# Attention with exponentials over three PSUM banks, transposes on VectorE and projections inside the loop

## The chip, the cores and the metric

The kernel runs on one core of a Trainium2 chip. The metric is the time of one launch in device microseconds (us). The engines are named as in the profile: PE (TensorE, with PEld for its weight loads), DVE (VectorE), ACT (ScalarE), POOL (GpSimd) and SP (the queue that issues most DMAs). Each engine runs its own instructions in order and waits on semaphores for the others. SBUF holds the data, PSUM (8 banks of 512 fp32 columns in each of 128 partitions) takes what PE computes.

## The reference

Six sublayers follow each other on an input x of 2 x 1024 x 128; only the first three matter here.

```python
x = x + 0.5 * _L0_ffn_ref(_layernorm(x), ...)    # routed cross attention
x = x + _L0_attn_ref(_layernorm(x), W_kqv, W_proj, q_norm_w, k_norm_w)
x = x + 0.5 * _L0_ffn_ref(_layernorm(x), ...)    # the same layer again
x = x + 0.5 * _L1_ffn_ref(...); x = x + _L1_attn_ref(...); x = x + 0.5 * _L1_ffn_ref(...)

# _L0_attn_ref, B=2, T=1024, H=16 heads of D=8
scores = jnp.einsum('bhtd,bhsd->bhts', q, k) / jnp.sqrt(jnp.float32(D))
scores = jnp.where(causal[None, None], -jnp.inf, scores)
att = jax.nn.softmax(scores, axis=-1)
y = jnp.einsum('bhts,bhsd->bhtd', att, v)
return y.transpose(0, 2, 1, 3).reshape(B, T, C) @ W_proj.T

# _L0_ffn_ref: the rows that each of 4 groups works on are chosen by a router
q_top, q_idx = jax.lax.top_k(q_logits, NQ);   queries = x[bidx, q_idx]
kv_top, kv_idx = jax.lax.top_k(kv_logits, NK); key_values = x[bidx, kv_idx]
```

## The kernel before

The program is written by hand: each engine has a list of instructions in a fixed order, and semaphores between them. `kinds` lists the sublayers; `attn(i)` and `ffn(i)` exist once for each engine. `ps` is the whole PSUM.

**The attention loop.** For each batch entry b (2) and each group hg of four heads (4), twelve steps run in the order of `ORDER` (L347). A step is one block of 128 keys (kt) against one half of the queries (qc, 512 of them), for four heads. Blocks on the causal diagonal are narrower: 512, 384, 256 or 128 queries (`SPAN`). There are 8 such groups of 12 steps. In a step:

- PE computes the scores (L1854, key on the partition, query along the row), two heads side by side on 64 rows each. They go to PSUM in fills of two banks, and three sets of two banks (banks 0 to 5) take turns. A full step has two fills, a narrow one (256 or 128) one.
- ACT takes the exponential of a fill (L1450) into the tile `P`, which holds 3 steps of 4 x 512. It waits for the scores of that fill and for the product three steps earlier (`pvs`), which frees its place.
- POOL zeroes what the causal mask forbids in diagonal blocks (L563).
- PE multiplies with the values (L1871), four heads side by side on 32 columns each, and adds up in bank 6 or 7. The values carry a column of ones, so the sum of the exponentials comes with it.

Here and below I call L1871 the product of a step. PE issues the scores two steps ahead: scores(s+2), then the product of s. When a unit (b, hg, qc) is complete, DVE copies its bank out (L1203), PE transposes it back (L1878), and DVE divides by the sums (L1206, L1208) into `Y`. After the loop, the four chunks of 512 tokens are transposed by PE (L1893), copied by ACT (L1453), projected by PE (L1898), and DVE adds them to X (L1215) and takes the statistics of the rows (L638, L641), one chunk after the other. The next layer starts from these.

**The gather in ffn.** The chosen rows are gathered by matmuls with one-hot matrices S. For each of 16 tiles of 128 tokens, DVE makes the 4 x 128 columns of the queries by comparing (L782), from `iota1` and `posT`, both in SBUF. The 4 x 64 columns of the keys take three instructions: a difference on POOL (L501), then an absolute value (L1324) and a relu (L1319) on ACT. PE waits for both and runs four matmuls (L1669): two parts of x, each against the queries and the keys.

Of the kernel before, what the change touches and what calls it, by code (L numbers as in the profile page):

```python
# [83 lines left out]
def _tiles():  # L84
    wide, order = 0, []
    for n in range(NNARROW):
        order.append((HT * NWIDE + n, 1))
        for _ in range(RUNS[n] if n < len(RUNS) else 0):
# [28 lines left out]
by_act = lambda t: t % 2 == 1  # L117
SIGNALS = {
# [3 lines left out]
                xn_high=2 * NC, xn_parts=NC, posTs=1, kdiff=NT, kabs=NT, Sk=NT, sig=2),  # L122
# [6 lines left out]
def build(nc, a, out, n_sub, start=0):  # L129
    ctx = ExitStack()  # L130
    with ctx:
# [77 lines left out]
        def rounded(name, at_word, shape):  # L209
# [64 lines left out]
        v = carve(head + [("P", 3 * HG * HALF), ("yT", 2 * HALF), ("Y", NT * D), ("tmp", 2 * P),  # L274
                          ("mx", 3 * TB * AH), ("msp", 3 * T // 2), ("mrest", T), ("rc", 2 * 16)])
        Pa = v["P"].rearrange("p (i h q) -> p i h q", i=3, h=HG)
        yT = v["yT"].rearrange("p (i q) -> p i q", i=2)
        Y = v["Y"].rearrange("p (t d) -> p t d", t=NT)
        YT = v["P"][:, 0:B * T]
        tmp = v["tmp"].rearrange("p (i q) -> p i q", i=2)  # L280
        mx = v["mx"].rearrange("p (k t h) -> p k t h", k=3, t=TB)
        rc = v["rc"].rearrange("p (i t h) -> p i t h", i=2, t=4)
# [64 lines left out]
        ORDER = ((0, 0), (1, 0), (0, 1), (1, 1), (0, 2), (1, 2), (0, 3), (1, 3), (1, 7), (1, 4), (1, 6), (1, 5))  # L347
        assert sorted(ORDER) == [(qc, kt) for qc in range(QC) for kt in range(4 * qc + 4)]
        STEPS = [(b, hg, qc, kt, all(q != qc for q, _ in ORDER[n + 1:]))
                 for b in range(B) for hg in range(NHG) for n, (qc, kt) in enumerate(ORDER)]  # L350
        SPAN = [HALF - P * max(0, kt - 4 * qc) for _, _, qc, kt, _ in STEPS]
        TURNS = [[(0, 1)] if n <= HALF // 2 else [(0,), (1,)] for n in SPAN]
        FILLS = [sum(len(x) for x in TURNS[:n]) for n in range(len(STEPS) + 1)]
        DIAG = [sum(kt >= 4 * qc for _, _, qc, kt, _ in STEPS[:n]) for n in range(len(STEPS) + 1)]
        ENDS = [n + 1 for n, x in enumerate(STEPS) if x[4]]
        UNIT = [sum(x[4] for x in STEPS[:n]) for n in range(len(STEPS) + 1)]

# [117 lines left out]
        def _(pool):  # L475
# [4 lines left out]
            def ffn(i):  # L480
# [16 lines left out]
                for t in range(NT):  # L497
                    if t >= 8:
                        pool.wait_ge(*at("Sk", i, t - 7))
                    j, r = spot(t)  # L500
                    nc.gpsimd.tensor_tensor(KD[:, t % 8], iota1[:, 0:NK].unsqueeze(1).broadcast_to([P, G, NK]),  # L501
                                            posT[:, j, r + G:r + 2 * G].unsqueeze(2).broadcast_to([P, G, NK]),
                                            ALU.subtract).then_inc(sem("kdiff", i), 1)
# [47 lines left out]
            def attn(i):  # L551
# [6 lines left out]

                for s_, (b, hg, qc, kt, last_) in enumerate(STEPS):
                    if kt >= 4 * qc:  # L560
                        pool.wait_ge(*at("exp", i, FILLS[s_ + 1]))
                        blk = Pa[:, s_ % 3, :, 0:P]
                        nc.gpsimd.affine_select(out=blk, in_=blk, pattern=[[0, HG], [1, P]], compare_op=ALU.is_ge,  # L563
                                                fill=0.0, base=0, channel_multiplier=-1).then_inc(sem("causal", i), 1)
# [60 lines left out]
        def _(dve):  # L625
# [89 lines left out]
            def ffn(i):  # L715
# [64 lines left out]
                for t in range(NT):  # L780
                    j, r = spot(t)
                    nc.vector.tensor_tensor(  # L782
                        S[:, t // TB, t % TB, 0:G * NQ].rearrange("p (g s) -> p g s", g=G),
                        iota1.unsqueeze(1).broadcast_to([P, G, NQ]),
# [290 lines left out]
            def attn(i):  # L1075
# [122 lines left out]
                for u in range(UNIT[-1]):  # L1198
                    b, hg, qc = u // (NHG * QC), u // QC % NHG, u % QC
                    dve.wait_ge(*at("pvs", i, ENDS[u]))  # L1200
                    if u >= 2:
                        dve.wait_ge(*at("yTt", i, u - 1))
                    nc.vector.tensor_copy(yT[:, u % 2, :], ps[:, 6 + u % 2, :]).then_inc(sem("yT", i), 1)  # L1203
# [8 lines left out]
                for c in range(NC):  # L1212
# [5 lines left out]
                    if i < last:  # L1218
                        row_stats(c, i + 1)
# [950 lines left out]
```

## Time and profile before

| | us |
|---|---|
| median of 3 runs | 814.76 (814.21 to 816.13) |
| profiled execution, its own time | 813.59 |
| its span in the trace | 811.8 |
| attention loop, first exponential to the end of the last | 170.8 to 309.0 |
| gather of the first ffn, its matmuls | 47.8 to 63.8 |
| gather of the second ffn, its matmuls | 357.6 to 373.5 |

The span is what the instructions of the trace cover; 1.8 us lie around it. Busy times of an engine count overlapping instructions once. A row of the timeline merges consecutive instructions of one line. Because instructions are pipelined, one starts before the end of the last, so what one more of them costs is read from the distance of two starts and not from its duration.

### The profile page before, as it was taken

What the parts mean: (1) busy time and instruction counts of PE and PEld (TensorE: products, weight loads), DVE (VectorE), ACT (ScalarE), POOL (GpSimd) and SP (SyncE); (2) the same over time, 40 slices, a digit from 0 to 9 for tenths busy, and PEclk for the clock granted to TensorE, in tenths of its full rate; (3) what the DMA queues carried; (4) which work ended last, traced back from release to release, by engine and by line L of the source; (5) the groups of instructions that cost most, each with busy time, mean ns of one, the idle gap of its engine ahead of it and who ended that gap; (6) DMA issues with size and microseconds to landing.
All of it is one profiled execution on the core that took longest, in us unless ns stands there. A gap on an engine that the chain in (4) does not pass through costs nothing. (4 is left out here: it accounts for less than half of the span.)

```text
span 811.8 us, 13446 instructions
## 1 busy us (share of the span) xinstructions
PE 641.5 (79%) x4710; PEld 468.1 (58%) x4710; DVE 459.0 (57%) x1401; ACT 441.7 (54%) x847; POOL 336.2 (41%) x422
## 2 busy tenths in 40 slices
PE   6879777479999998049877599999729758999990
PEld 3757574222222224036567589999628747999980
DVE  7894859931111115985747545556556783555572
ACT  5565534579999995536544444444424373444440
POOL 1173343203332221256150657765431046677553
PEclk9689999569999999559998789999959967999996
DMA  8220000668000000002000576667330028666654
GB/s 327 95 73 35 1 2 0 207 213 305 6 2 1 2 1 1 1 4 104 1 1 8 148 252 217 214 190 203 110 103 1 1 63 291 209 217 194 192 162 161
DMA packets 36470, 87.60 MB, mean 108 GB/s; under 512 B 5169, under 2 KB 20145, under 8 KB 35377
## 3 DMA queue, kind: packets, MB, share of 16 engines
q1 hardware_dynamic: 31280, 76.13, 28.5%
q0 software_dynamic: 5120, 10.58, 4.6%
q8 instruction: 39, 0.64, 0.3%
q14 instruction: 31, 0.25, 0.1%
HBM read 69.75 MB, written 16.94 MB: 107 GB/s over the span
## 5 line engine op out<-in xcount | busy, mean ns | idle before, releaser
L1959 PE MATMUL ps<-arena 128*128 128x256 f32 (+1 forms) x768 | 156.8, 356 | 2.3 <-issue 1.2
L1505 ACT ACTIVATE arena<-ps,arena 128x256 f32<-128x256 f32 (+1 forms) x192 | 84.1, 438 | 129.1 <-issue 76.5
L1959 PEld LDWEIGHTS ps<-arena 128*128 128x128 f32 x768 | 129.9, 196 | 19.0 <-issue 3.4
L1450 ACT ACTIVATE arena<-ps 128x1024 f32<-128x1024 f32 (+2 forms) x160 | 135.8, 957 | 4.0 <-PE ps L1854 2.6
L975 DVE SCALAR_TENSOR_TENSOR arena<-ps,arena 128x256 f32<-128x256 f32 (+1 forms) x192 | 84.3, 440 | 82.3 <-ACT arena L1505 80.4
L611 POOL DMA_INDIRECT yd<-arena,wqk x80 | 78.6, 983 | 68.5 <-DVE arena L997 57.5
L575 POOL DMA_INDIRECT arena<-xs,wqk x80 | 77.6, 970 | 31.4 <-issue 15.2
L563 POOL TENSOR_SCALAR_AFFINE_SELECT arena<-arena 128x512 f32<-128x512 f32 x64 | 40.6, 635 | 111.8 <-ACT arena L1450 111.8
L1871 PE MATMUL ps<-arena 128*32 128x512 f32 (+3 forms) x768 | 83.3, 506 | 2.7 <-DVE arena L1208 1.6
L1970 PE MATMUL ps<-arena 128*128 128x128 f32 x640 | 79.5, 275 | 2.0 <-DVE arena L997 2.0
L1970 PEld LDWEIGHTS ps<-arena 128*128 128x128 f32 x640 | 75.2, 192 | 2.5 <-issue 2.4
L1203 DVE COPY arena<-ps 128x512 f32<-128x512 f32 x16 | 11.1, 692 | 96.6 <-PE ps L1871 96.6
L1854 PE MATMUL ps<-arena 64*128 64x512 bf16 (+3 forms) x384 | 52.9, 338 | 8.9 <-DVE arena L1132 4.2
L1854 PEld LDWEIGHTS ps<-arena 64*128 64x128 bf16 x384 | 13.5, 94 | 66.5 <-ACT arena L1450 48.6
L501 POOL TENSOR_TENSOR arena<-consts,arena 128x256 f32<-128x256 f32 x32 | 32.8, 1061 | 23.5 <-DVE arena L774 23.5
L1563 PE MATMUL ps<-consts 128*128 128x128 f32 x146 | 26.2, 361 | 18.1 <-DVE X L1009 16.4
L1563 PEld LDWEIGHTS ps<-consts 128*128 128x128 f32 x146 | 25.1, 271 | 18.6 <-DVE X L1009 16.6
L993 DVE TENSOR_TENSOR arena<-ps,arena 128x256 f32<-128x256 f32 (+1 forms) x48 | 18.3, 380 | 26.1 <-PE ps L1970 25.7
L1871 PEld LDWEIGHTS ps<-arena 128*32 128x32 f32 x768 | 15.7, 108 | 30.0 <-issue 15.2
L782 DVE TENSOR_TENSOR S<-consts,arena 128x512 fp32r<-128x512 f32 x32 | 32.0, 1072 | 0.1
L1256 ACT ACTIVATE Xn<-X,rt 128x128 f32<-128x128 f32 x72 | 29.0, 479 | 1.2 <-DVE rt L693 1.2
L581 POOL TENSOR_SCALAR wvo<-wqk,wvo 128x24 f32<-128x24 f32 x2 | 0.7, 356 | 67.9 <-DVE wvo L928 67.9
(297 smaller groups left out, 1184.6 us busy)
## 6 DMA issues: line engine op xcount, KB each, us to landing
arena<-in_wall SPq DMA_DIRECT2D x48, 836.0 KB, 4.6
arena<-slots SPq DMA_DIRECT2D x2, 2048.0 KB, 7.2
arena<-scr_q SPq DMA_DIRECT2D x8, 512.0 KB, 6.6
arena<-scr_k SPq DMA_DIRECT2D x8, 512.0 KB, 7.7
arena<-yd SPq DMA_DIRECT2D x8, 512.0 KB, 5.5
xs<-Xn SPq DMA_DIRECT2D x8, 260.0 KB, 5.2
scr_q<-arena SPq DMA_DIRECT2D x4, 384.0 KB, 4.4
scr_k<-arena SPq DMA_DIRECT2D x4, 384.0 KB, 4.0
```

Of the source, the lines that this page charges most:

```text
L501: nc.gpsimd.tensor_tensor(KD[:, t % 8], iota1[:, 0:NK].unsqueeze(1).broadcast_to([P, G, NK]), posT[:, j, r + G:r + 2 * G].unsqueeze(2).bro ...
L563: nc.gpsimd.affine_select(out=blk, in_=blk, pattern=[[0, HG], [1, P]], compare_op=ALU.is_ge, fill=0.0, base=0, channel_multiplier=-1).then ...
L575: nc.gpsimd.indirect_dma_start(out=xt[:, slot, h, :], out_offset=None, in_=xs, in_offset=bass.IndirectOffsetOnAxis(ap=tokidx[:, col + h:co ...
L611: nc.gpsimd.indirect_dma_start(out=yd, out_offset=bass.IndirectOffsetOnAxis(ap=dest[:, col + h:col + h + 1], axis=0), in_=y_[:, slot, h, : ...
L975: nc.vector.scalar_tensor_tensor(out=hT[:, j % 2, f, 0:rows], in0=ps[:, 3 + k % 3, 0:rows], scalar=raw[:, slot, EW_BB + f:EW_BB + f + 1], ...
L1450: nc.scalar.activation(dst, src, ACT.Exp, scale=AD ** -0.5).then_inc(sem("exp", i), 1)
L1505: nc.scalar.activation(sl[:, k % 3, 0:rows], ps[:, k % 3, 0:rows], ACT.Silu, bias=raw[:, slot, EW_BA + f:EW_BA + f + 1]).then_inc(sem("sil ...
L1563: mm(ps[:, bank, 0:P], ident, ident, start=True, stop=True)
L1854: ins = mm(ps[:, 2 * (k % 3) + par, n * x:n * (x + 1)], Ks[64 * par:64 * par + R_ALL, h2, T * b + P * kt:T * b + P * (kt + 1)], Qs[64 * pa ...
L1871: ins = mm(ps[32 * j:32 * j + 32, 6 + u % 2, q0:HALF], Va[:, TB * b + kt, VW * h:VW * h + 32], Pa[:, s_ % 3, j, 0:HALF - q0], start=(kt == ...
L1959: ins = mm(ps[:, bank, 0:rows], raw[:, slot, w + P * f:w + P * (f + 1)], xTt[:, j % 2, 0:rows], start=True, stop=True)
L1970: ins = mm(ps[:, 6, D * h:D * (h + 1)], hT[:, j % 2, f, P * h:P * (h + 1)], raw[:, slot, EW_2 + D * f:EW_2 + D * (f + 1)], start=(f == 0), ...
```

## The change

Four things change in attention.

- Steps may hold two key blocks. `ORDER` has ten steps for each group, and the blocks 384+128 wide share a step. Each step takes whole banks of 512 columns: four banks, or two where the block is 256 wide. The 36 banks of a group are filled in 12 fills of three banks, regardless of where a step ends. Two sets of three banks (0 to 2, 3 to 5) take turns.
- One ACT instruction takes the exponential of 3 x 512 columns; there are 96 instead of 160. The tile `P` is as large as before, now a ring of 12 banks. `FREED` says how many products must be done before a fill may be written into it.
- PE issues scores(k+2), which wait for exponential k to be complete, and after them the products of the steps whose last bank was in fill k-1.
- A finished unit is transposed by DVE in blocks of 32 x 32, from PSUM to SBUF (L1242), divided there, and once the last group of heads is in, DVE transposes the blocks back (L1252) into the operand of the projection; the rows of W_proj are permuted on the host to match. PE transposes nothing in attention, ACT copies nothing after the loop. Chunks 0, 1 and 2 are projected and added to X inside the loop, at places given by `PROJECT_AFTER`; chunk 3 after it.

In ffn, PE puts `iota1` into PSUM bank 6, and DVE compares from there. For three of the 16 tiles (4, 9, 14) DVE makes the key columns too, so POOL and ACT make 13.

```diff
+KEYS_DVE = (4, 9, 14)
+KEYS_ACT = [t for t in range(NT) if t not in KEYS_DVE]
...
-        ORDER = ((0, 0), (1, 0), (0, 1), (1, 1), (0, 2), (1, 2), (0, 3), (1, 3), (1, 7), (1, 4), (1, 6), (1, 5))
...
+        ORDER = ((0, (0,)), (0, (1, 3)), (1, (0,)), (1, (1,)), (0, (2,)), (1, (6,)), (1, (4,)), (1, (2,)), (1, (5, 7)), (1, (3,)))
...
+        FILL, RING = 3, 3 * HG
+        NFILL = len(BANKS) // FILL
+        SCORE_FILLS = 6 // FILL
...
+        LAST_FILL = [max(n for n, (m, _) in enumerate(BANKS) if m == s_) // FILL for s_ in range(len(STEPS))]
+        FREED = [sum(n <= FILL * k + FILL - 1 - RING for n in FIRST_BANK) for k in range(NFILL)]
...
+        ADD_AT = [QC * NHG - 2, QC * NHG, UNITS - 2, UNITS - 1]
+        PROJECT_AFTER = [min(ENDS[u] + 3, len(STEPS) - 1) for u in ADD_AT[:-1]]
...
                     nc.vector.tensor_tensor(
                         S[:, t // TB, t % TB, 0:G * NQ].rearrange("p (g s) -> p g s", g=G),
-                        iota1.unsqueeze(1).broadcast_to([P, G, NQ]),
+                        ps[:, 6, 0:P].unsqueeze(1).broadcast_to([P, G, NQ]),
...
-                    nc.vector.tensor_copy(yT[:, u % 2, :], ps[:, 6 + u % 2, :]).then_inc(sem("yT", i), 1)
...
+                    nc.vector.transpose(yq[:, u % 2, :], ps[:, 6 + u % 2, :]).then_inc(sem("yq", i), 1)
...
+                        nc.vector.transpose(YT[:, HALF * c:HALF * (c + 1)], yn[:, qc, :]).then_inc(sem("YT", i), 1)
+                    if u in ADD_AT:
+                        add_projected(ADD_AT.index(u))
...
-                for s_, (b, hg, qc, kt, last_) in enumerate(STEPS):
-                    n = SPAN[s_]
-                    for k, us in enumerate(TURNS[s_], FILLS[s_]):
-                        act.wait_ge(*at("sT", i, k + 1))
-                        if s_ >= 3:
-                            act.wait_ge(*at("pvs", i, s_ - 2))
...
+                for k in range(NFILL):
+                    act.wait_ge(*at("sT", i, k + 1))
+                    if FREED[k]:
+                        act.wait_ge(*at("pvs", i, FREED[k]))
+                    n0, bank = FILL * k % RING, FILL * (k % SCORE_FILLS)
+                    nc.scalar.activation(Pa[:, n0:n0 + FILL, :], ps[:, bank:bank + FILL, :], ACT.Exp, scale=AD ** -0.5
+                                         ).then_inc(sem("exp", i), 1)
...
+                def scores(k):
+                    banks = BANKS[FILL * k:FILL * (k + 1)]
+                    if k >= SCORE_FILLS:
+                        pe.wait_ge(*at("exp", i, k - SCORE_FILLS + 1))
...
+                for k in range(SCORE_FILLS):
+                    scores(k)
+                for k in range(NFILL):
+                    if k + SCORE_FILLS < NFILL:
+                        scores(k + SCORE_FILLS)
+                    for s_ in range(len(STEPS)):
+                        if LAST_FILL[s_] == k - 1:
+                            attend(s_)
+                for s_ in range(len(STEPS)):
+                    if LAST_FILL[s_] == NFILL - 1:
+                        attend(s_)
+                attended(NC - 1)
```

**PE inside the loop**, at the change from the first group of heads to the second. `ps<-arena 128x512` is a score matmul, `ps<-arena 32x512` one of a product. Before, a step's scores, with a wait for an exponential at each fill of two banks, stand between two products:

```order
L1871 MATMUL ps<-arena 32x512 [waits attn_exp]
L1871 MATMUL ps<-arena 32x512 x3
L1854 MATMUL ps<-arena 128x128 [waits attn_exp]
L1854 MATMUL ps<-arena 128x128 x3
L1871 MATMUL ps<-arena 32x256 [waits attn_causal,attn_exp]
L1871 MATMUL ps<-arena 32x256 x3
L1854 MATMUL ps<-arena 128x512 [waits attn_exp]
L1854 MATMUL ps<-arena 128x512
```

Of the changed kernel, PE in the same place:

```order
L1889 MATMUL ps<-arena 128x512 [waits attn_exp]
L1889 MATMUL ps<-arena 128x512 x2
L1889 MATMUL ps<-arena 128x512 [waits attn_stack_01,attn_exp]
L1889 MATMUL ps<-arena 128x512 x2
L1912 MATMUL ps<-arena 32x512 [waits attn_exp]
L1912 MATMUL ps<-arena 32x512 x3
L1889 MATMUL ps<-arena 128x512 [waits attn_exp]
L1889 MATMUL ps<-arena 128x384 x2
L1889 MATMUL ps<-arena 128x128 x2
L1912 MATMUL ps<-arena 32x384 [waits attn_causal,attn_exp]
L1912 MATMUL ps<-arena 32x384 x3
L1912 MATMUL ps<-arena 32x128 x4
```

A score fill is now three matmuls (or more, narrow ones) behind one wait, and sometimes two fills stand between two products. No product stands between the wait for exponential k and the scores of fill k+2; the products come behind them.

**ACT at the start of the loop**, before:

```order
L1450 ACTIVATE arena<-ps 128x1024 [waits attn_sT,attn_split]
L1450 ACTIVATE arena<-ps 128x1024 [waits attn_sT] x3
L1450 ACTIVATE arena<-ps 128x2x384 [waits attn_sT] x2
L1450 ACTIVATE arena<-ps 128x1024 [waits attn_pvs,attn_sT] x2
L1450 ACTIVATE arena<-ps 128x2x2x256 [waits attn_pvs,attn_sT]
```

and of the changed kernel, with what stands ahead of the loop:

```order
L1452 ACTIVATE arena<-ps,attw 128x512 [waits attn_kqT]
L1456 ACTIVATE arena<-arena 128x512 [waits attn_rest] x2
L1483 ACTIVATE arena<-ps 128x1536 [waits attn_sT,attn_split]
L1483 ACTIVATE arena<-ps 128x1536 [waits attn_sT] x3
L1483 ACTIVATE arena<-ps 128x1536 [waits attn_pvs,attn_sT] x92
```

Four forms of two banks have become one form of three banks. Both wait for `pvs`; the number that it waits for is in `FREED`.

**PE behind the loop**, before, from the last product to the first transposes of the next layer (the pair of rows L1893 and the pair L1898 stand four times each):

```order
L1871 MATMUL ps<-arena 32x384 [waits attn_causal,attn_exp]
L1871 MATMUL ps<-arena 32x384 x3
L1878 MATMUL ps<-consts,arena 128x128 [waits attn_yT]
L1878 MATMUL ps<-consts,arena 128x128 x3
L1893 MATMUL ps<-consts,arena 128x128 [waits attn_Y]
L1893 MATMUL ps<-consts,arena 128x128 x3
```

and of the changed kernel:

```order
L1912 MATMUL ps<-arena 32x512 [waits attn_exp]
L1912 MATMUL ps<-arena 32x512 x3
L1920 MATMUL ps<-attw,arena 128x128 [waits attn_yq,attn_YT]
L1920 MATMUL ps<-attw,arena 128x128 x3
L1589 MATMUL ps<-consts,X 128x128 [waits x_chunk]
L1589 MATMUL ps<-consts,X 128x128 x3
```

One projection is left behind the last product, and directly after it the 16 transposes of the next layer.

## Rows read from the trace of the kernel before

**Rows 1.** The page of the profile: the costliest group of ACT: busy us, mean ns | idle before.

```profile
L1450 ACT ACTIVATE arena<-ps 128x1024 f32<-128x1024 f32 (+2 forms) x160 | 135.8, 957 | 4.0 <-PE ps L1854 2.6
```

**Rows 2.** Windows: stretch, length, busy us of each engine (instructions), granted clock, DMA.

```profile
170.00:178.30 8.30, 7.19 (x32) 1.13 (x32) 0.00 (x1) 6.86 (x8) 1.27 (x2) 0.50 0.90 290
178.30:309.00 130.70, 125.16 (x1176) 34.16 (x1172) 18.61 (x45) 128.92 (x153) 38.70 (x61) 1.00 0.18 62
...
196.00:213.10 17.10, 16.32 (x154) 4.46 (x152) 2.48 (x6) 16.93 (x21) 5.08 (x8) 1.00 0.44 162
```

**Rows 3.** ACT in the attention loop: start, duration, line, tile, forms, count.

```profile
170.77 5.18 ACT L1450 ACTIVATE arena<-ps 128x1024 f32<-128x1024 f32 x6 [1.49 <-PE ps L1854]
...
179.02 129.98 ACT L1450 ACTIVATE arena<-ps 128x1024 f32<-128x1024 f32 x152 [0.46 <-PE ps L1854]
...
201.38 0.61 ACT L1450 ACTIVATE arena<-ps 128x512 f32<-128x512 f32 x1
...
201.86 1.05 ACT L1450 ACTIVATE arena<-ps 128x1024 f32<-128x1024 f32 x1
...
207.10 1.06 ACT L1450 ACTIVATE arena<-ps 128x1024 f32<-128x1024 f32 x1
...
208.00 1.07 ACT L1450 ACTIVATE arena<-ps 128x1024 f32<-128x1024 f32 x1
```

**Rows 4.** PE in one group: start, duration, line, tile, count, idle before it.

```profile
205.67 0.61 PE L1854 MATMUL ps<-arena 64*128 64x512 bf16 x4
206.21 0.64 PE L1871 MATMUL ps<-arena 128*32 128x256 f32 x8
...
209.13 0.34 PE L1854 MATMUL ps<-arena 64*128 64x384 bf16 x2 [0.39 <-ACT arena L1450]
209.39 1.07 PE L1871 MATMUL ps<-arena 128*32 128x512 f32 x8
210.39 0.66 PE L1878 MATMUL ps<-consts,arena 128*128 128x128 f32 x4
```

**Rows 5.** The timeline behind the loop: DVE and PE.

```profile
310.76 0.69 DVE L1203 COPY arena<-ps 128x512 f32<-128x512 f32 x1 [3.93 <-PE ps L1871]
...
312.20 0.26 DVE L1206 RECIPROCAL arena<-ps 128x16 f32<-128x16 f32 x1 [0.75 <-PE ps L1878]
...
312.49 0.29 DVE L1208 TENSOR_TENSOR arena<-ps,arena 128x128 f32<-128x128 f32 x1
...
313.77 3.74 PE L1898 MATMUL ps<-attw,arena 128*128 128x128 f32 x32
...
320.99 0.69 DVE L1215 TENSOR_TENSOR X<-X,ps 128x512 f32<-128x512 f32 x1
...
325.95 0.42 DVE L726 TENSOR_TENSOR arena<-arena,ps 128x256 f32<-128x256 f32 x1 [0.29 <-ACT arena L1284]
```

**Rows 6.** The gather: timeline of the second ffn, L782 in the first, L1093, a window.

```profile
354.41 16.00 DVE L782 TENSOR_TENSOR S<-consts,arena 128x512 fp32r<-128x512 f32 x16
354.46 16.42 POOL L501 TENSOR_TENSOR arena<-consts,arena 128x256 f32<-128x256 f32 x16 [17.79 <-DVE arena L774]
...
L782 DVE TENSOR_TENSOR S<-consts,arena x15: 1095/1097/1101, 45.3 to 59.5; 128x512 fp32r<-128x512 f32 x15
...
L782 DVE TENSOR_TENSOR S<-consts,arena x2: 691/896/1101, 44.6 to 45.3; 128x512 fp32r<-128x512 f32 x2
...
L1093 DVE TENSOR_TENSOR arena<-ps,consts x16: 410/414/426, 127.9 to 155.6; 128x256 f32<-128x256 f32 x16
...
357.50:362.50 5.00, 4.91 (x15) 4.26 (x16) 5.00 (x6) 4.03 (x10) 5.00 (x6) 0.50 0.01 3
...
363.45 0.53 PE L1669 MATMUL ps<-S,xn_high 128*128 128x512 f32 x2
...
363.81 0.51 PE L1669 MATMUL ps<-S,xn_low 128*128 128x512 f32 x2
...
373.01 0.51 PE L1669 MATMUL ps<-S,xn_low 128*128 128x512 f32 x2
```

More of the change, by code:

```diff
@@ L351, in build @@
[L351 to L354, printed above, removed]
+        ORDER = ((0, (0,)), (0, (1, 3)), (1, (0,)), (1, (1,)), (0, (2,)), (1, (6,)), (1, (4,)), (1, (2,)), (1, (5, 7)), (1, (3,)))
+        assert sorted((qc, kt) for qc, kts in ORDER for kt in kts) == [(qc, kt) for qc in range(QC) for kt in range(4 * qc + 4)]
@@ new lines, in build @@
+        STEPS = [(b, hg, qc, kts, all(q != qc for q, _ in ORDER[n + 1:]))
+                 for b in range(B) for hg in range(NHG) for n, (qc, kts) in enumerate(ORDER)]
+        first_query = lambda qc, kt: P * max(0, kt - 4 * qc)
+        span = lambda qc, kt: HALF - first_query(qc, kt)
+        BANKS = []
+        for s_, (b, hg, qc, kts, last_) in enumerate(STEPS):
+            if span(qc, kts[0]) == HALF // 2:
+                BANKS += [(s_, [(par, kts[0], 0), (2 + par, kts[0], HALF // 2)]) for par in range(2)]
+            else:
+                BANKS += [(s_, [(j, kt, span(qc, kts[0]) * n) for n, kt in enumerate(kts)]) for j in range(HG)]
@@ L557, in attn @@
                     nc.gpsimd.tensor_tensor(kq[:, t, :], kq[:, t, :], rot[:, t % 2, :], ALU.add).then_inc(sem("kq", i), 1)
-                for s_, (b, hg, qc, kt, last_) in enumerate(STEPS):
[L560 to L564, printed above, removed]
+                for s_, (b, hg, qc, kts, last_) in enumerate(STEPS):
+                    if masked(s_):
+                        pool.wait_ge(*at("exp", i, LAST_FILL[s_] + 1))
+                        half = span(qc, kts[0]) == HALF // 2
+                        n0 = FIRST_BANK[s_] % RING
+                        for n in range(len(kts)):
+                            col = 3 * P * n
+                            blk = (Pa[:, n0:n0 + 2, :].rearrange("p j (u q) -> p (j u) q", u=2)[:, :, 0:P] if half
+                                   else Pa[:, n0:n0 + HG, col:col + P])
+                            ins = nc.gpsimd.affine_select(out=blk, in_=blk, pattern=[[0, HG], [1, P]], compare_op=ALU.is_ge,
+                                                          fill=0.0, base=0, channel_multiplier=-1)
+                        ins.then_inc(sem("causal", i), 1)
             def moe(i):
@@ L1665, in ffn @@
                         pe.wait_ge(*at("S", i, t + 1))
[L1666 removed]
+                        pe.wait_ge(*at("Sk", i, sum(m <= t for m in KEYS_ACT)))
                         for part in range(2):
@@ L1869, in pv @@
[L1869 to L1872 removed]
+                    if 0 in kts and u >= 2:
+                        pe.wait_ge(*at("yq", i, u - 1))
+                    if 0 in kts and u - 2 in ADD_AT:
+                        pe.wait_ge(*x_of(i + 1, ADD_AT.index(u - 2)))
@@ new lines, in pv @@
+                    where = {(j, kt): (FIRST_BANK[s_] % RING + x, col)
+                             for x, (m, pieces) in enumerate(BANKS[FIRST_BANK[s_]:FIRST_BANK[s_] + HG]) if m == s_
+                             for j, kt, col in pieces}
+                    for kt in kts:
+                        for j in range(HG):
+                            h = HG * hg + j
+                            n, col = where[j, kt]
+                            ins = mm(ps[32 * j:32 * j + 32, 6 + u % 2, first_query(qc, kt):HALF], Va[:, TB * b + kt, VW * h:VW * h + 32],
+                                     Pa[:, n, col:col + span(qc, kt)], start=(kt == 0), stop=last_ and kt == kts[-1])
```

175 lines of the change are left out of this document (79 added, 96 removed).

## The prediction

> **What bounds the kernel now.** I read the costliest groups first. The exponentials are 160 instructions and 135.8 us busy [rows 1], one sixth of the span. Then the windows: from 178.3 to 309.0 us ACT is busy 128.92 of 130.70 us, PE 125.16 [rows 2]. In one group of heads (196.0 to 213.1) ACT has 16.93 of 17.10 us, PE 16.32 [rows 2]. So ACT sets the pace of the loop and PE follows closely. The loop runs from 170.77 to 179.02 + 129.98 = 309.00 us, 138.2 us [rows 3].
>
> What does one exponential cost? Two of 1024 columns start 0.90 us apart (207.10, 208.00), one of 512 columns is followed after 0.48 (201.38, 201.86) [rows 3]. The difference, 0.42 us for 512 columns, is 0.83 ns a column; what is left for an instruction is 0.05 us. The duration of one is longer, 1.05 to 1.07 us at 1024 and 0.61 at 512 [rows 3]: it goes on in the pipeline after the next has begun, and only its end releases the others.
>
> **Attention loop: ACT's part.** The columns stay the same (18,432 for a group, 147,456 in all). At three banks an exponential starts every 0.90 + 0.42 = 1.32 us (I take 1.33, with the digits behind the rounding), and lasts 1.05 + 0.42 = 1.47. A group is 12 x 1.33 = 16.0 us, against 17.1 now. If nothing else mattered, that would give back 1.1 us eight times, 9 us.
>
> **Attention loop: the new wait.** Something else matters. The ring holds four fills. Fill k+2 is written where fill k-2 was, and `FREED` wants the product of the step that began there. In every case but two in a group this is a product that PE issues in iteration k, behind scores(k+2), and these wait for exponential k to be complete. Thus a chain leads from exponential k to exponential k+2. Its parts:
> - exponential k from start to end, 1.47 us;
> - until PE starts, 0.06: the exponential that starts at 208.00 ends at 209.07, PE starts at 209.13 [rows 3, 4];
> - three score matmuls. Four, in two pairs side by side, take 0.54 (205.67 to 206.21) [rows 4]. Three need two turns of the array as well, so 0.54;
> - the product at 512 columns, 1.07 from start to the last end (209.39); the next starts after 1.00 (210.39) [rows 4];
> - until ACT starts, 0.05, a hop of the same kind as the 0.06.
>
> Sum 3.19 us, where ACT alone would need 2 x 1.33 = 2.66: ACT waits 0.5 us. I went through a group's 12 fills this way. Where products stand in three iterations in a row (twice in a group), PE is the limit all through: 1.53 + 3 x 0.54 + 3.2 for three products (1.0 each, 1.15 with two blocks) + 0.05 = 6.4 us for what ACT does in 5.3, so 1.1. Two single cases cost 0.5 each; behind the two-bank steps nothing waits. That makes 3.2 us, and a group takes 16.0 + 3.2 = **19.2 us instead of 17.1**. The same bookkeeping with the order of the kernel before gives 16.9 a group where the trace has 17.1, so it is low if anything.
>
> Over eight groups: 8 x 19.2 = 153.6. Three projections now stand in PE's queue inside the loop. One is 3.74 / 4 = 0.93 us [rows 5], and PE is on the chain, so I add 0.8 each, 2.4. The start runs at half clock (granted 0.50 until 178.3, where PE is busy 7.19 of 8.30 us [rows 2]); before, ACT's first eight exponentials there took 8.25 us instead of about 7, so +1.2 before and I take +1.6 now. The first fill is one matmul later, 0.3. Less 1.0 for the places at which a projection falls into a wait. Sum 156.9 against 138.2: **+18.7 us**. Bounds: +13 if the projections and the half clock cost nothing and each gate is 0.1 smaller; +21 if ACT loses another 0.3 a group by restarting.
>
> What of the chain is covered: the masks (one select on POOL is under the next exponential; the double one, 1.3 us, is ready before PE has written the next scores), and DVE's work per unit, which is idle most of the time.
>
> **Behind the loop.** Before, the last product's result is taken up at 310.76, chunk 3 is added from 320.99, and the first DVE operation of the routing that needs the next layer's logits starts at 325.95 [rows 5]. Now: transpose on DVE, for which no row exists. Nearest is the copy of the same tile, 0.69 [rows 5]; I take 0.75, with 0.69 and 1.4 (two passes) as ends. Then 0.26 + 0.29 for the division [rows 5], 0.75 for the second transpose, 0.15 of links, 0.95 for the projection, 0.1: the addition starts 3.2 us after the product instead of 10.2, a gain of 7.0. Three things go against this: the last two products now end 2.2 us after the last exponential instead of 1.7 (0.5); PE does all 16 transposes and the logits of the next layer behind the last projection, where before they ran between the additions, about 0.8 more until the routing starts. Net **-5.7 us** (-4 to -6.5).
>
> **The gather.** DVE and POOL run in lockstep here: 16 comparisons in 16.00 us, 16 differences in 16.42 [rows 6]. The first comparison, which started before POOL, took 0.69 us, the 15 others 1.10 [rows 6]. So they exclude each other while both read two SBUF operands. A DVE operation with one operand in PSUM keeps 0.41 us at 256 columns in all 16 cases, between 127.9 and 155.6 us, where POOL works too [rows 6]. So DVE gets to about 0.6 a tile, POOL to at most 0.72, ACT's two operations at 0.7, and 13 of them. PE becomes the bound: at full clock a tile is two parts 0.36 apart (363.45, 363.81), 0.71; at half clock (357.5 to 362.5, granted 0.50, 16 weight loads in 5.0 us) 1.25 [rows 6]. Second ffn: PE starts 0.8 earlier, at 356.8; until 362.5 it does 4.5 tiles, then 11.5 x 0.71 = 8.2, end 370.7 instead of 373.5 [rows 6]: -2.8. First ffn, the half clock being shorter: -3.6. Sum **-6.4 us**, with 0 (DVE and POOL still exclude each other) and -10 (clock full all through) as ends. DVE's three extra key tiles (0.35 each) are under PE. The matmul that puts `iota1` in PSUM is under DVE's scan.
>
> **Sum.** +18.7 - 5.7 - 6.4 = **+6.6 us** on the profiled 813.6, 820.2; the median of the runs lies 1.2 above that execution, so 821.4.
>
> A rule speaks for the change. The Trainium skill, page "ScalarE: Activation LUTs", section "Rules for kernel authors", budgets about 0.3 us for each ACTIVATE besides 0.83 ns an element. The slope agrees with the rows above. By its fixed part, 64 instructions fewer would be worth 19 us, and the loop would end near 119 us instead of 157. The spacing of the starts contradicts that for instructions in a row: 0.05 us.
>
> **Rivals.**
> 1. *ACT stays the bound.* If ring and sets never made it wait, the loop would take 8 x 16.0 + 1.2 = 129 us, -9; with the other terms 814.8 - 9 - 5.7 - 6.4 = 794. For it: PE's busy 16.32 us of a group [rows 2] lose two transposes of 0.66 [rows 4], so its load fits below 16.0. If each of the 64 instructions saved were worth the whole part of its duration that is not columns (1.05 - 0.85 = 0.2 us), that is 13 us and about the same, 790. Against it: the chain above is latency, not load, and its parts have rows. 6%, of which 1% for the price of 0.2. The skill's 0.3 us would put it at 784.
> 2. *The gates are half as long*, because PE's third score matmul or the product's end is cheaper than I take it. Loop +8, total 811. Faster by a little. 9%.
> 3. *The loop is as computed and the gather gains nothing*, the exclusion being there with a PSUM operand as well: 828. 9%.
> 4. *The clock.* PE waits more (some 80% busy instead of 95%), and could be granted 0.5 for a stretch in the loop. Each 3.4 us of it costs some 3: 825 to 835. 5%.
> 5. *Between*: loop +14, the rest at its better ends: 814 to 816. 11%.
> The forecast, 817 to 826 with its own bounds: 60%.
>
> **Numbers.** About 0.2% (1.6 us) is what a measurement tells from no change. Faster (below 813.1): cases 1 and 2, 15%. Same: case 5, 11%. Slower: the rest, 74%. The range, 813 to 829, leaves out case 1, most of case 2 and the far end of 4.
>
> **What would show it.** In the trace after: exponentials of 1536 columns lasting 1.45 to 1.5 us and ACT idle before many of them, released by L1912 (the product) rather than by the scores; idle in about 9 of 12; a group in 19 us; loop 155 to 158 us; the addition of chunk 3 about 6 us after the last exponential; comparisons at 0.6 us; gather matmuls ending 3 us earlier. Wrong if a group takes 16 to 17 us with ACT dense, or if the transpose on DVE takes more than 1.4 us.

## The result, and the profile after

| | kernel before | changed kernel |
|---|---|---|
| median, lowest to highest of the runs | 814.5 (813.8 to 816.1) | 826.8 (820.3 to 828.5) |
| profiled execution: time, span | 813.6, 811.8 | 826.6, 824.8 |
| ratio of the times, 95% interval | | 1.0133 (1.0076 to 1.019) |

The changed kernel is slower by 12.3 us. The spans of the two traces differ by 13.0 us, and the stretches below add up to that without a remainder. Every boundary is the start or the end of an instruction in the trace. A gather is counted here from its first comparison on DVE to its last matmul.

| stretch | before | after | difference |
|---|---|---|---|
| start to the first comparison of the first gather | 44.6 | 47.2 | +2.6 |
| first gather, to its last matmul | 19.1 | 13.6 | -5.5 |
| to the first exponential | 107.0 | 107.4 | +0.4 |
| attention loop, to the end of the last exponential | 138.2 | 158.3 | **+20.1** |
| to the addition of chunk 3 | 12.0 | 5.9 | -6.1 |
| to the first comparison of the second gather | 33.4 | 34.9 | +1.5 |
| second gather | 19.1 | 16.4 | -2.7 |
| to the end (nothing in it is changed) | 438.2 | 440.9 | +2.7 |

**The loop.** The page's group of the exponentials, which answers to [rows 1]; columns busy us, mean ns, then idle time before them and what ended it:

```profile
L1483 ACT ACTIVATE arena<-ps 128x1536 f32<-128x1536 f32 x96 | 135.5, 1449 | 24.7 <-PE ps L1912 21.5
```

The idle time was 4.0 us and is now 24.7, and 21.5 of it ends with L1912, the product. The busy time has hardly changed (135.8, 135.5). Windows of the changed kernel, for [rows 2]: its slow start, the rest of the loop, one group of heads. A line has the stretch and its length, the busy time (instructions) of PE, PEld, DVE, ACT and POOL, the granted clock, the busy share of the DMA engines and GB/s.

```profile
168.20:178.30 10.10, 8.30 (x49) 1.82 (x45) 0.00 (x0) 7.00 (x6) 1.86 (x3) 0.52 0.91 321
178.30:326.60 148.30, 122.21 (x1104) 33.43 (x1099) 25.21 (x67) 128.55 (x91) 37.98 (x61) 1.00 0.13 47
208.84:228.23 19.39, 15.82 (x147) 4.10 (x144) 2.52 (x6) 16.97 (x13) 4.98 (x8) 1.00 0.00 1
```

A group takes 19.39 us, and neither ACT (16.97) nor PE (15.82) fills it: both are busy for a smaller share of the time than before ([rows 2]: 16.93 and 16.32 of 17.10). So the time is set by a chain of waits and not by the load of an engine. The timeline shows it link by link, ACT first and then PE, with start and duration (an ACT line holds two exponentials; where it lasts 2.99 and not 2.79, the second one started 0.2 late as well):

```profile
208.84 2.99 ACT L1483 ACTIVATE arena<-ps 128x1536 f32<-128x1536 f32 x2 [0.44 <-PE ps L1912]
212.07 2.79 ACT L1483 ACTIVATE arena<-ps 128x1536 f32<-128x1536 f32 x2 [0.24 <-PE ps L1912]
215.30 2.99 ACT L1483 ACTIVATE arena<-ps 128x1536 f32<-128x1536 f32 x2 [0.44 <-PE ps L1912]
```

```profile
213.57 0.60 PE L1889 MATMUL ps<-arena 64*128 64x512 bf16 x3 [1.09 <-ACT arena L1483]
214.11 1.06 PE L1912 MATMUL ps<-arena 128*32 128x512 f32 x8
215.10 0.60 PE L1889 MATMUL ps<-arena 64*128 64x512 bf16 x5
```

The exponential from 212.07 lasts 1.45, to 213.52. The scores start 0.05 later and are issued in 0.54. The product runs from 214.11 to 215.17, and 0.13 later, at 215.30, ACT starts the exponential after the next. The sum, 1.45 + 0.05 + 0.54 + 1.06 + 0.13, is 3.23 us. The three lines of ACT are 3.23 apart each, and six such steps are the group: 6 x 3.23 = 19.39.

**Behind the loop.** DVE and PE, for [rows 5]:

```profile
328.74 0.72 DVE L1242 STREAM_TRANSPOSE arena<-ps 128x512 f32<-128x512 f32 x1 [0.40 <-PE ps L1912]
329.49 0.25 DVE L1245 RECIPROCAL arena<-arena 128x16 f32<-128x16 f32 x1
329.78 0.29 DVE L1246 TENSOR_TENSOR arena<-arena 128x128 f32<-128x128 f32 x1
330.10 0.71 DVE L1252 STREAM_TRANSPOSE arena<-arena 128x512 f32<-128x512 f32 x1
...
332.49 0.69 DVE L1233 TENSOR_TENSOR X<-X,ps 128x512 f32<-128x512 f32 x1 [1.67 <-PE ps L1920]
```

```profile
330.87 1.58 PE L1920 MATMUL ps<-attw,arena 128*128 128x128 f32 x8 [2.26 <-DVE arena L1252]
```

**The gather.** DVE and POOL in the second ffn, for [rows 6], and two windows: the first gather and the second.

```profile
367.43 2.48 DVE L814 TENSOR_TENSOR S<-ps,arena 128x512 fp32r<-128x512 f32 x4
369.83 0.41 DVE L810 TENSOR_TENSOR S<-ps,arena 128x256 fp32r<-128x256 f32 x1
370.16 3.07 DVE L814 TENSOR_TENSOR S<-ps,arena 128x512 fp32r<-128x512 f32 x5
```

```profile
367.47 7.47 POOL L522 TENSOR_TENSOR arena<-consts,arena 128x256 f32<-128x256 f32 x13 [18.36 <-DVE arena L801]
```

```profile
367.43:383.83 16.40, 14.18 (x64) 12.10 (x64) 11.73 (x26) 10.28 (x28) 11.78 (x15) 0.74 0.27 105
47.21:60.85 13.64, 11.38 (x64) 9.69 (x64) 11.73 (x26) 11.04 (x30) 9.10 (x14) 1.00 0.33 124
```

Comparisons start 0.60 us apart instead of 1.02, differences 0.57 (7.47 / 13). The lockstep is gone, and PE is the bound: in the second gather its last matmul ends 5.7 us after DVE's last comparison (3.1 before). With the clock granted in full the gather takes 13.6 us, with a part of it at half clock (0.74 on average) 16.4.

### The profile page after: what moved, and what is told of

Same layout as the page of the kernel before. It is cut to its first block and busy times, and to the rows that moved or that the text cites. A ratio compares the mean times of both kernels' runs of the same rounds, so it can differ in the third digit from the quotient of the medians.

```text
span 824.8 us, 13133 instructions
## 1 busy us (share of the span) xinstructions
PE 633.1 (77%) x4634; PEld 467.9 (57%) x4634; DVE 448.3 (54%) x1411; ACT 432.3 (52%) x767; POOL 317.6 (39%) x416
## 5 line engine op out<-in xcount | busy, mean ns | idle before, releaser
L1483 ACT ACTIVATE arena<-ps 128x1536 f32<-128x1536 f32 x96 | 135.5, 1449 | 24.7 <-PE ps L1912 21.5
L1889 PE MATMUL ps<-arena 64*128 64x512 bf16 (+3 forms) x384 | 59.9, 339 | 31.8 <-ACT arena L1483 25.4
L1912 PE MATMUL ps<-arena 128*32 128x512 f32 (+3 forms) x768 | 78.2, 504 | 0.4 <-ACT arena L1483 0.4
L1242 DVE STREAM_TRANSPOSE arena<-ps 128x512 f32<-128x512 f32 x16 | 11.5, 717 | 119.3 <-PE ps L1912 119.3
L1889 PEld LDWEIGHTS ps<-arena 64*128 64x128 bf16 x384 | 15.6, 95 | 92.1 <-ACT arena L1483 77.0
L1594 PE MATMUL ps<-consts 128*128 128x128 f32 x146 | 24.9, 348 | 18.0 <-DVE X L1041 16.4
L1912 PEld LDWEIGHTS ps<-arena 128*32 128x32 f32 x768 | 17.9, 109 | 34.1 <-issue 33.5
L1594 PEld LDWEIGHTS ps<-consts 128*128 128x128 f32 x146 | 23.8, 258 | 18.5 <-DVE X L1041 16.5
L1287 ACT ACTIVATE XT<-ps 128x512 f32<-128x512 f32 x24 | 13.7, 597 | 27.6 <-PE ps L1589 27.4
L1384 ACT ACTIVATE arena<-ps,arena 64x512 f32<-64x512 f32 x32 | 21.8, 682 | 11.2 <-PE ps L1754 8.4
```

Of the source, the lines that this page charges most:

```text
L1483: nc.scalar.activation(Pa[:, n0:n0 + FILL, :], ps[:, bank:bank + FILL, :], ACT.Exp, scale=AD ** -0.5).then_inc(sem("exp", i), 1)
L1594: mm(ps[:, bank, 0:P], ident, ident, start=True, stop=True)
L1889: ins = mm(ps[:, FILL * (k % SCORE_FILLS) + x, col:col + span(qc, kt)], Ks[lo:lo + R_ALL, h2, T * b + P * kt:T * b + P * (kt + 1)], Qs[lo: ...
L1912: ins = mm(ps[32 * j:32 * j + 32, 6 + u % 2, first_query(qc, kt):HALF], Va[:, TB * b + kt, VW * h:VW * h + 32], Pa[:, n, col:col + span(qc ...
```

## The experiments

All times are medians. The kernel before ran beside each batch, at 813.9, 814.9 and 814.9 us, and the ratios are to it.

**1. A longer ring.** Is the wait for the product what costs, and does it go with one more fill or two? The banks of P go from 12 to 18, in memory that four other tiles used at other times. DVE waits once, ahead of its first transpose, so that those tiles are done with.

```diff
-        FILL, RING = 3, 3 * HG
+        FILL, RING = 3, 18
...
-        v = carve(head + [("P", 3 * HG * HALF), ("yq", 2 * HALF), ("yn", QC * HALF), ("YT", B * T), ("tmp", 2 * P),
-                          ("mx", 3 * TB * AH), ("msp", 3 * T // 2), ("mrest", T), ("rc", 2 * 16)])
+        v = carve(head + [("P", 18 * HALF), ("yq", 2 * HALF), ("yn", QC * HALF), ("YT", B * T), ("rc", 2 * 16)])
+        v |= carve([("tmp", 2 * P), ("mx", 3 * TB * AH), ("msp", 3 * T // 2), ("mrest", T)], v["P"])
...
+                dve.wait_ge(*at("scr", i, 16 * 4 * len(SAME) * B))
```

> The changed kernel, with a ring of 18 banks (six fills) for the exponentials instead of 12 (four); the order of the matmuls, the two sets of three PSUM banks, the forms of all instructions and the columns are the same. The gate theory (exponential k+2 waits for a product that stands behind the wait for exponential k): the product that frees the place is then four fills old and done, so ACT runs at its own pace but for the moments where PE is late. A group of heads takes 16.5 to 16.8 us instead of 19.4, the loop 135 to 139 us instead of 158.3, the whole 805 us (10 below the kernel before). Rival A, PE's load (a fill of three banks leaves half of a pair of matmuls empty) sets the pace: nothing changes, group 19.4. Rival B, the two sets of PSUM banks are the wait (the scores of k+2 come too late): nothing changes either, ACT released by the scores instead of by the product.

Measured: 801.3 us, ratio 0.985 (0.978 to 0.993). Loop 135.0. One group in a window, and the page's group of the exponentials:

```profile
201.84:218.06 16.22, 15.61 (x150) 4.11 (x144) 2.62 (x6) 16.22 (x13) 5.05 (x9) 1.00 0.00 1
```

```profile
L1484 ACT ACTIVATE arena<-ps 128x1536 f32<-128x1536 f32 x96 | 130.7, 1461 | 6.2 <-PE ps L1890 5.8
```

ACT is busy all 16.22 us, and nothing waits for a product any more: what idle time is left ends with the scores. The ring alone is worth 23 us in the loop. The group came out below the 16.5 to 16.8 expected, and the whole below 805.

**2. The control.** The same memory, the same added wait, 18 banks, but `FREED` as for 12. Against the kernel of experiment 1:

```diff
-        FREED = [sum(n <= FILL * k + FILL - 1 - RING for n in FIRST_BANK) for k in range(NFILL)]
+        FREED = [sum(n <= FILL * k + FILL - 1 - 3 * HG for n in FIRST_BANK) for k in range(NFILL)]
```

> Control for the ring of 18 banks: its layout of SBUF, its 18 banks and its one added wait, but FREED as for 12 banks, so that only the waits of the ring of 12 come back. Theory A (the wait of scores for the product, through FREED, is the whole loss): group 19.4, loop 158, total 824 to 828, as the changed kernel. Theory B (the layout, or what stands in the same addresses, did the gain of the ring of 18): group near 16.3, total 801.

Measured: 823.9 us, ratio 1.015 (1.010 to 1.020). A group again takes 19.39 us, the loop 158.6, and the idle time before the exponentials is 24.9, of which 21.8 ends with the product. One number in `FREED` carries the whole loss of the loop, and the layout carries none of it.

**3. How much more ring?** 15 banks in the place of 18. A group has 36 banks, which 15 does not divide. The kernel leaves out the wrap of the ring inside a step: some steps begin at bank 12, 13 or 14 and read and mask on into banks 15 to 17, which no exponential fills, so those products, and all that follows from them, use other numbers. The count and the size of the instructions stay as they were, so the length of the loop can be compared; the total is less sure, since the later layers choose their rows from these numbers.

> The ring of 18 banks cut to 15, that is one fill more than the changed kernel's 12; everything else as in the kernel with 18. Theory A (the chain runs through the product of the same iteration; one fill more lets the gate ask for a product that PE has issued before the scores, and then ACT sets the pace): group 16.2 to 16.5, loop 135, total 801 to 803, the same as with 18. Theory B (each bank gives back a part of the wait): group about 17.8, half way between 19.4 and 16.2, loop 147, total 813.

Measured: 798.1 us, ratio 0.980 (0.975 to 0.985). Loop 134.8, a group 16.22. One more fill is enough, and a second one brings nothing more in the loop. It is a threshold and not a slope: with 12 banks `FREED` asks in 8 of the 12 fills of a group for a product of the same iteration, with 15 or 18 in none.

**4. A shorter distance.** The changed kernel with the gate of a ring of 9:

```diff
-        FREED = [sum(n <= FILL * k + FILL - 1 - RING for n in FIRST_BANK) for k in range(NFILL)]
+        FREED = [sum(n <= FILL * k + FILL - 1 - (RING - FILL) for n in FIRST_BANK) for k in range(NFILL)]
```

> The changed kernel with FREED as if its ring were one fill smaller (9 banks), no other line touched: the gate then asks for a product that stands behind the exponential just before. Theory A (the gate's distance in fills is what sets the group): exponential, product and scores come one behind the other in most places, 1.45 + 0.06 + 1.0 + 0.54 + 0.05 = 3.1 us for one or two exponentials; a group about 31 us, loop 240 to 250, total 905 to 920. Theory B (the gate is passed before it matters and the loss is something else, for instance exponentials of 1536 columns being slow by themselves): loop near 158, total 825 to 830.

Measured: 970.8 us (two executions), ratio 1.191, well above what either theory gave. Loop 307.7. ACT's timeline at two places, and windows over two stretches:

```profile
284.49 1.45 ACT L1483 ACTIVATE arena<-ps 128x1536 f32<-128x1536 f32 x1 [3.08 <-PE ps L1912]
289.02 2.79 ACT L1483 ACTIVATE arena<-ps 128x1536 f32<-128x1536 f32 x2 [3.08 <-PE ps L1912]
...
331.00 1.45 ACT L1483 ACTIVATE arena<-ps 128x1536 f32<-128x1536 f32 x1 [1.78 <-PE ps L1912]
334.24 1.45 ACT L1483 ACTIVATE arena<-ps 128x1536 f32<-128x1536 f32 x1 [1.79 <-PE ps L1912]
```

```profile
240.00:300.00 60.00, 40.51 (x213) 7.93 (x209) 3.96 (x9) 23.25 (x17) 6.85 (x11) 0.53 0.00 1
...
284.49:289.02 4.53, 2.89 (x13) 0.48 (x13) 0.06 (x1) 1.45 (x1) 0.00 (x0) 0.50 0.00 0
```

At full clock (1.00 from 331.00 to 334.24) a step is 334.24 - 331.00 = 3.24 us, the same chain as above, now mostly for one exponential where it was for two. But over most of the loop the granted clock was 0.5 (0.62 on average from 180 to 420 us), PE waiting for ACT in every step, and there the step is 4.53 us. The chain's price at full clock was near what I expected (3.1). What was left out is that with this gate PE was also granted less clock, which made the chain longer again. It is the prediction's rival 4, and it did not occur in the changed kernel, where the clock is 1.00 from 178.3 to the end of the loop.

**5. Products ahead of scores.** The changed kernel, with the order in PE's queue turned round:

```diff
                 for k in range(NFILL):
-                    if k + SCORE_FILLS < NFILL:
-                        scores(k + SCORE_FILLS)
                     for s_ in range(len(STEPS)):
                         if LAST_FILL[s_] == k - 1:
                             attend(s_)
+                    if k + SCORE_FILLS < NFILL:
+                        scores(k + SCORE_FILLS)
```

> The changed kernel with one edit in PE's order: in iteration k the products of the steps ending in fill k-1 stand ahead of scores(k+2) instead of behind them. Ring and sets as they are. Gate theory: the product no longer waits for exponential k, only for k-1 and for the mask; where the mask takes one select, ACT isn't stopped; where it takes two (1.3 us), PE is held and the scores come late instead. A group takes 17.6 us, the loop 145 us, the whole 813 to 815. Rival A (PE's load): no change, 826. Rival B (sets too few): no change or slower, since the scores come later still.

Measured: 806.4 us, ratio 0.990 (0.986 to 0.993). Loop 141.2, most groups 17.5. The group is what was expected (17.6), the loop and the whole are shorter (145 and 813 to 815 expected). The gate no longer counts, but a group is 1.3 us longer than with the long ring. Both remedies together say why:

> The ring of 18 banks and, on top, the products of step LAST_FILL = k-1 ahead of the scores of fill k+2. Theory A (with 18 banks ACT is the bound at 16.2 us a group = 12 x 1.35 and the order has nothing left to give): groups 16.2 to 16.9, loop 133 to 137, total 799 to 803. Theory B (the two remedies add, since each takes another part of the chain): total below 797. A third outcome, that the scores now come late behind two products and ACT waits for them: group 17.2 or more, total 805 or more.

Measured: 806.9 us, ratio 0.991 (0.988 to 0.995). The groups are those of the reordered kernel, 17.52 (loop 142.5, with a slower start). So the third outcome came: with this order the length of the ring does not matter, since the order has a wait of its own. POOL, PE and ACT where it stands:

```profile
200.45 1.23 POOL L589 TENSOR_SCALAR_AFFINE_SELECT arena<-arena 128x512 f32<-128x512 f32 x2 [3.39 <-ACT arena L1484]
```

```profile
201.83 1.07 PE L1913 MATMUL ps<-arena 128*32 128x384 f32 x16 [0.59 <-ACT arena L1484]
202.83 0.60 PE L1890 MATMUL ps<-arena 64*128 64x512 bf16 x5
```

```profile
203.47 5.68 ACT L1484 ACTIVATE arena<-ps 128x1536 f32<-128x1536 f32 x4 [0.40 <-PE ps L1890]
```

The double mask ends at 201.68, and the product starts at 201.83. The PE line names ACT, but by the code the product waits for this mask and for the exponential that the mask waits for too, and that one had ended at 200.39. The scores stand 1.0 us behind it, and ACT waits for them until 203.47. In the original order this mask is covered by the scores ahead of the product.

**6. The old loop with the rest of the change.** The gather's part alone, the transposes and projections alone (in the old loop with its twelve steps), and both. What was changed is named in the expectations.

> The kernel before with the gather's part of the change alone (comparisons from PSUM, three tiles' key columns on VectorE); attention as before. My working: 2.8 + 3.6 = 6.4 us less, 808 us; the gather of each ffn is bound by PE at 0.71 us a tile at full clock. Rival: VectorE and GpSimd still exclude each other with one operand in PSUM, then under 2 us less.

Measured: 804.2 us, ratio 0.988 (0.983 to 0.993). That is 9.7 us less, where 6.4 were expected; of the 8.4 us between the two traces 5.6 lie in the two gathers and 3.7 behind the second one, where no instruction differs.

> The kernel before with the transposes on VectorE and the projections of chunks 0 to 2 inside the loop; fills of two banks in three sets, twelve steps and the gather as before. Behind the loop 6 us less. In the loop PE loses the sixteen transposes (0.6 us each), on which ACT waited 0.6 us a group, 5 less, and gets three projections, 2 more: loop 135 instead of 138.2. In all 9 us less, 805.5. Rival: PE in the loop has no slack for the projections and each costs its whole 0.93 us or more, in all 4 us less.

Measured: 808.6 us, ratio 0.995 (0.992 to 0.998). Groups of 16.69 instead of 17.11 (PE no longer transposes), those with a projection 17.78, so a projection costs 1.09 in this loop. Loop 137.3. Chunk 3 is added 6.1 us after the last exponential ends. In all 5.3 us less, where 9 were expected: the loop gave back 0.9 us and not 3, for a group gained 0.42 and the projections took most of that again.

> The kernel before with both other parts of the change (the gather's two hunks, and the transposes on DVE with the chunks projected in the loop), but with the old exponentials over one or two banks and the old twelve steps. Theory A (the parts add, the new exponentials alone make the loss): 814.5 - 9.7 - 5.3 = 799.5, between 797 and 802; loop 137 to 138 us, groups of 16.7 and 17.8; the changed kernel then loses 27 us by its sets of three banks, of which the loop itself shows 158.3 - 137.3 = 21. Theory B (the parts overlap, since both pull the same clock or the same wait forward): 803 to 806.

Measured: 801.1 us, ratio 0.987 (0.982 to 0.992). Loop 136.9. The parts add within the interval (799.5 from the two alone). The changed kernel is 26 us slower than this one, of which its loop shows 21.4. With the ring of 18 the exponentials over three banks come to the same total, 801.3. Per group they save 0.47 us (16.22 against 16.69), but the first group, part of it at half clock, takes 19.06 against 17.83, so the loops differ by 1.9 us.

**7. Which half of the gather's part?** Once only the operand in PSUM, with all 16 tiles of keys on POOL and ACT; once only the three tiles on DVE, with the other comparisons from SBUF. Each is shown against the kernel with the gather's whole part:

```diff
-KEYS_DVE = (4, 9, 14)
+KEYS_DVE = ()
```

```diff
-                        ps[:, 6, 0:P].unsqueeze(1).broadcast_to([P, G, NQ]),
+                        iota1.unsqueeze(1).broadcast_to([P, G, NQ]),
```

> The kernel before with the gather's one operand of DVE read from PSUM (iota1 put there by a matmul), but all 16 tiles of keys left to POOL and ACT (KEYS_DVE empty). Theory A (DVE and POOL exclude each other only while both read two operands in SBUF; the PSUM operand alone ends it): comparisons 0.6 us, differences 0.57, PE or ACT the bound with 16 tiles of about 0.75, so the gather ends 2 to 3 us earlier than before twice, total 808 to 810, most of the 9.7 us of both gather hunks together. Theory B (the three tiles moved from POOL and ACT to DVE are what gains): comparisons stay at 1.0 to 1.1 us, total 813 to 815.

> The other half of the gather's hunks: three of sixteen tiles of keys on DVE, whose comparisons read iota1 from SBUF as before (the three key comparisons read PSUM). Theory A (lockstep stays while both read two operands in SBUF): comparisons of 512 columns 1.0 to 1.1 us, differences 1.0 to 1.1, DVE 16 x 1.07 + 3 x 0.4 = 18.3 instead of 17.1 us, no gain in the gather or up to 1 us lost in each, total 813 to 817. Theory B (fewer tiles for POOL and ACT are worth something by themselves): gather 2 us shorter each, total 808 to 810.

Measured: 805.9 us, ratio 0.990 (0.986 to 0.993), and 805.6 us, ratio 0.990 (0.986 to 0.993). By their times these two and the whole gather part (804.2) can't be told apart. The traces can, counted from the first comparison to the last gather matmul:

| | first gather | second gather |
|---|---|---|
| before | 19.1 | 19.1 |
| three tiles on DVE only | 16.7 | 16.8 |
| PSUM operand only | 13.8 | 16.3 |
| both (gather's part alone) | 16.4 | 16.3 |
| both (changed kernel) | 13.6 | 16.4 |

Where DVE reads PSUM, the clock decides between the values: 13.6 and 13.8 stand at a granted clock of 1.00, 16.3 and 16.4 at 0.74 to 0.79. So rows are compared only at like clocks.

```profile
350.50 13.36 POOL L503 TENSOR_TENSOR arena<-consts,arena 128x256 f32<-128x256 f32 x13 [18.48 <-DVE arena L776]
```

```profile
348.27 9.18 POOL L503 TENSOR_TENSOR arena<-consts,arena 128x256 f32<-128x256 f32 x16 [18.49 <-DVE arena L776]
```

The first line is with the three tiles only: 13 differences in 13.36 us, still in lockstep. The second is with the PSUM operand only: 16 in 9.18, no lockstep. So theory A holds for the PSUM operand. It failed for the three tiles, for which I had expected no gain: the lockstep does stay, but POOL and ACT are done three tiles earlier and the last matmuls no longer wait for them (the last one ends 1.3 us after DVE's last comparison, before it was 3.1). With the PSUM operand in place the three tiles bring 0.2 us at most at full clock (13.6 against 13.8), and nothing at 0.75 (16.3 both).

## Why the prediction came out as it did

The direction was right, and the time lies in the range: 821.4 forecast, 826.8 measured, 813 to 829 allowed. The size of the change came out at about twice the forecast: +6.6 us forecast, +12.3 measured (+13.0 between the traces). The three terms of the sum come to +7.3, and even that near match owes something to luck, since the gather's error (-1.8) takes up most of those of the loop (+1.4) and of what follows it (+1.1). By its steps:

**Attention loop, +18.7 forecast, +20.1 measured.** The mechanism was as described, and experiments 1 to 4 show it: a gate that reaches a product of the same iteration. The prediction counted such gates in all fills of a group but two; `FREED` has them in eight of twelve, and it is before these eight that ACT starts late (about nine forecast). The sum for the chain was 3.19 us and it is 3.23. One link was mis-sized, the hop from the product's end to ACT, 0.05 forecast and 0.13 measured. A plain exponential is followed after 1.33 to 1.35, as forecast. A group is 19.39 instead of 19.2, since the waits of a group come to six such chains, each 0.04 longer than forecast. Over eight groups that is 1.5 us, all that the term missed. A projection costs 0.93 in the two full groups that have one (20.32), 0.8 forecast. The first group is 1.76 longer than the others, for which I took 1.6.

**Behind the loop, -5.7 forecast, -4.6 measured** (-6.1 to the addition, +1.5 from there to the gather). The addition comes 5.9 us after the last exponential, about 6 forecast. The block transpose takes 0.72 us where I took 0.75, for want of a row. The addition starts 3.8 us after DVE takes up the product (328.74 to 332.49) instead of 3.2, mostly because the projection took 1.58 and not 0.95. The clock had fallen there:

```profile
331.00:334.10 3.10, 3.10 (x17) 3.10 (x18) 1.56 (x5) 0.60 (x1) 0.00 (x0) 0.57 0.00 0
```

**The gather, -6.4 forecast, -8.2 measured** (-5.5 and -2.7). For the second the sum was right to 0.1 us: from the first comparison to the end, 16.3 forecast, 16.4 measured. For the first I took half clock for a stretch of it, and it had the full clock all through. That mis-sized term is 1.9 us. Neither figure is a property of the change alone. In the kernels with this same gather the first took 13.6 to 16.4 us and the second 14.9 to 16.4, by where the half clock fell (granted 1.00 down to 0.74), so the match of the second to 0.1 us is luck in part.

**The stretches that the change does not touch.** The three terms make +7.3 us in place of +6.6. The rest of the 13.0, 5.7 us, lies outside them: +2.6 ahead of the first gather, +0.4 between it and the loop, +2.7 behind the second gather. I had put these at nothing. The only new instruction there is the matmul that puts `iota1` into PSUM, ahead of the first gather, and it can't account for 2.6 us: in six of the ten other kernels that have it the first comparison starts at 43.8 to 44.3 us, no later than before. It starts at 47.1 to 47.8 in three of the eleven, the changed kernel among them, and these have the lowest mean clock up to there (0.78 to 0.79, the others 0.81 to 0.88). Windows from the end of the second gather to the end of the program, of before, of the changed kernel and of the gather's part alone:

```profile
373.50:811.80 438.30, 356.07 (x2477) 320.14 (x2476) 256.42 (x826) 184.64 (x425) 212.76 (x252) 0.90 0.44 136
```

```profile
383.80:824.80 441.00, 355.93 (x2477) 320.27 (x2476) 254.33 (x826) 184.68 (x425) 209.88 (x251) 0.90 0.44 136
```

```profile
368.80:803.40 434.60, 352.54 (x2477) 317.81 (x2476) 253.43 (x826) 184.58 (x425) 209.79 (x251) 0.91 0.44 138
```

The same 2477 matmuls take 434.6 to 441.0 us, and the shortest stretch goes with the highest mean clock. So it is over all thirteen traces, whose kernels have the same code there: 433.8 us at 0.92 (the ring of 15, with its other numbers), 434.6 to 437.3 at 0.91, 438.2 to 440.9 at 0.90. That the clock is the cause is argued and not shown, since no run moved it alone. It is no fixed property of a kernel either: the changed kernel's own four runs went from 820.3 to 828.5 us, at mean clocks from 0.901 to 0.887. So whether any of these 5.7 us belongs to the change stays open.

**The rivals.** Rival 1 (ACT stays the bound) is what the changed kernel does as soon as the ring is longer: 16.22 us a group where it said 16.0, but a loop of 135.0 and a total of 801.3 where it said 129 and 794, since it left out the projections (1.09 us in each of two groups) and took 1.2 us for a start that cost 2.8 (19.06 for the first group). Rivals 2 and 5 (a shorter wait) failed with the chain of 3.23 us. Rival 3 failed: the comparisons are at 0.60. Rival 4 did not happen in the changed kernel, and experiment 4 shows what it costs when it does. The Trainium skill, page "ScalarE: Activation LUTs", section "Rules for kernel authors", budgets about 0.3 us for each ACTIVATE whose bias is a pointer operand. The exponentials here are given no bias, a condition that the prediction left out when it drew on the row. With the long ring, where ACT has no idle time inside a group, eight fewer of them brought 0.47 us a group against the old loop, or 0.06 for each instruction saved. For these exponentials in a row the trace stands against the 0.3; even the duration of one, 1.45 us, is only some 0.2 above 1536 columns at 0.83 ns.

## What to carry to other kernels

When instructions over a ring are made larger while the ring keeps its size, count the ring in fills and not in banks: here 12 banks were enough at two banks a fill and one fill short at three, and that alone cost 23 us. Before merging instructions to save their fixed cost, take that cost from the spacing of two that follow each other without a wait, and write down the chain from one use of a buffer to the next; if its length over the number of fills it spans is above the engine's pace, the chain sets the time. Here it was 3.23 us over two fills, 1.62 a fill, where ACT alone needs 1.35. A busy share that falls on both engines of a loop, with the idle time ended by one line, is the sign of it.

## What the runs showed of the hardware

- A transpose on DVE of 128 x 512 f32 in blocks of 32 x 32 takes 0.72 us from PSUM and 0.71 from SBUF, as much as an addition of the same tile (0.69).
- DVE's comparisons and POOL's differences held each other up while DVE read both operands from SBUF, 1.02 us a comparison and 1.03 a difference (13.36 / 13), and not with one of DVE's in PSUM, 0.60 and 0.57.
- A loop in which PE waited in every step was granted half clock for most of its length (0.53 from 240 to 300 us in experiment 4). The changed kernel's loop kept 1.00 from 178.3 us to its end (PE busy 122.21 of 148.30 us).
- Code that is the same to the last instruction took 434 to 441 us in thirteen kernels that differ only ahead of it, and one kernel's own runs lay 8 us apart. A difference below about 1% between two kernels, found from one trace of each, may lie wholly in stretches that neither changed.
